# TensorE multiplies the identity by itself while it waits in three layer norms of a four-layer stack

## The chip, the cores and the metric

One NeuronCore of a Trainium2 chip runs the whole program in one launch. The metric is device time in microseconds (us), the median over runs.

## What is computed

Four layers act on x, 16 sequences of 256 tokens with 128 channels, in float32. Each layer normalises x, puts the result through a mixer s and a feed-forward part g, and adds the gated product:

```python
xn = _layernorm(x, axis=-1)
s = mixer(xn)          # delta rule, recurrence, local attention, causal attention
g = _silu(ffn(xn))     # layers 0 and 3: gated experts; 1 and 2: experts on chosen tokens
x = x + s * g
```

Layer 0's feed-forward part has an attention of its own, a norm (ln1), and eight experts of which the two best count. Layer 2 assigns tokens to eight experts by `norm @ centroids.T`. Layer 3 routes by `xt @ gate_w.T`. So three norms are followed at once by a product with a small routing matrix of 6 or 8 columns.

## The kernel before, in words

The program is a sequence of stages. `phase` opens a block in which each engine has its own list of instructions, and closes it with a barrier of all engines; engines wait for each other through semaphores (`wait_ge`, `then_inc`). 4096 tokens lie as 32 blocks of 128 (tokens on partitions); a norm takes them in 8 groups (GRP) of 4 blocks (GB).

`layer_norm` (L272) builds such a stage out of the class `Norm`. Per group: ACT opens the gate with silu (`open_gate`, L199) where the norm also adds the layer's product to x; DVE combines and takes statistics (`statistics`, L161 to L209); POOL takes the root (`root`, L215 and L216); DVE makes the bias (`centre`, L220); ACT normalises (`normalize`, L228, four instructions); TensorE transposes the four blocks into a PSUM bank, two banks in turn (`turn`, L243); ACT (`save_ch`, L248) or, with `columns`, DVE (`save_scaled`, L253) saves the bank to channel-major form; TensorE multiplies it with the routing matrix (`route`, L263); at the end DVE copies all logits (`save_logits`, L269). On TensorE the order is written out by hand: transposes of group g, then routing products of group g-1. On DVE it is statistics of g, bias of g-1, save of g-2.

Two of the three norms are calls of `layer_norm` with a router: **l0n1** (called at L1387, layer 0's ln1, on the attention's output, no gate, `columns` given, so DVE saves) and **norm3** (L2807, before layer 3, with gate; each group's input is waited for in `landed`). The third is **n2**, the function `norm_and_norm` (L339), before layer 2. It has the same structure with lines of its own: gates L463, statistics L379 and L382, POOL's first root L414 and L415 and second root L420 to L423 (two norms in a row are folded into one), bias L387, normalise L468, transposes L438, save L474, routing products L445, a small product for an offset (L450), and the first reader of the logits (L403).

A fourth routing norm, norm1, runs inside the last groups of layer 0's experts; it is built from `Norm` directly and isn't touched. Behind l0n1 come those experts (`experts`, up-products L555), behind n2 layer 2's mixer, behind norm3 layer 3's attention, which opens with projections (L2910, L2911, L2914). Ahead of l0n1 stands the output projection of layer 0's mixer (L1272). The scan of that mixer has transposes at L1028 and small products at L1039.

The PSUM banks of a norm are two for the transposes and one tile for the logits.

Of the kernel before, what the change touches and what calls it, by code (L numbers as in the profile page):

```python
# [13 lines left out]
P = 128  # L14
# [11 lines left out]
@contextmanager  # L26
def phase(nc, names, steps=1, spent=()):

    with ExitStack() as ctx:
        sems = [ctx.enter_context(nc.semaphore(n)) for n in names]
        step = ctx.enter_context(nc.Fori(0, steps)) if steps > 1 else 0
        with nc.Block() as block:
            yield block, step, sems
        numbers = sorted(s.num for s in sems + list(spent))
        while numbers:
            run = 1
            while run < len(numbers) and numbers[run] == numbers[0] + run:
                run += 1  # L40
            nc.sync.sem_clear(range(numbers[0], numbers[0] + run))
            numbers = numbers[run:]
        nc.all_engine_barrier()  # L43
# [118 lines left out]
    return dve.tensor_tensor(st.x[:, rows, :], st.x[:, rows, :], gate, ALU.add)  # L162


class Norm:


# [104 lines left out]
def layer_norm(nc, c, name, src, dst, dst_ch=None, gain=None, shift=None, combined=None, fetch=(), fetched=None, router=None,  # L272
# [2 lines left out]
    AHEAD = 2  # L275
    with ExitStack() as ctx:
        n = Norm(nc, ctx, c, name, src, dst, dst_ch, gain, shift, combined, router, ready, columns=columns)
        with phase(nc, [name + "_dve_step", name + "_pool_step"], spent=n.sems + list(spent)) as (block, _, (dve_step, pool_step)):
            if fetch:
                @block.sync  # L280
                def _(sp):
                    for to, what in fetch:
                        sp.dma_start(to, what).then_inc(fetched, 16)
# [27 lines left out]
            if dst_ch is not None:  # L311
                @block.tensor
                def _(pe):
                    for g in range(GRP + 1):
                        if g < GRP:
                            n.turn(pe, g)
                        if router is not None and g >= 1:
                            n.route(pe, g - 1)

            @block.scalar  # L320
            def _(act):
# [17 lines left out]
def norm_and_norm(nc, c, st, second, columns, cent, score, fetch, fetched, ready, ffn, ffn_fetched, landed):  # L339

    E = cent.shape[1]
    with ExitStack() as ctx:
# [7 lines left out]
        shifts = mem.sb("n2_shifts", [P, P])  # L350
        offset = mem.sb("n2_offset", [P, E])
        pt = [mem.psum(f"n2_pt{n}", [P, GB, P]) for n in range(2)]
        logits = mem.psum("n2_logits", [P, BLK, E])
        p_offset = mem.psum("n2_p_offset", [P, E])
        names = ["n2_" + n for n in ("gate_ready", "stats_ready", "first_ready", "second_ready", "bias_ready", "norm_ready", "turned",
                                     "ch_saved", "cent_ready", "offset_ready", "routed", "dve_step", "pool_step")]
        with phase(nc, names, spent=landed) as (block, _, sems):
# [73 lines left out]
            @block.tensor  # L431
            def _(pe):
                def turn(g):
                    pe.wait_ge(norm_ready, g + 1)
                    if g >= 2:
                        pe.wait_ge(ch_saved, g - 1)
                    for j in range(GB):
                        ins = pe.transpose(pt[g % 2][:, j, :], st.xn[:, g * GB + j, :], c.ident[:, :])  # L438
                    ins.then_inc(turned, 1)

                def route(g):
                    pe.wait_ge(ch_saved, g + 1)
                    for j in range(GB):
                        b = g * GB + j
                        ins = pe.matmul(logits[:, b, :], st.xnt[:, b * P:(b + 1) * P], scaled[:, :], start=True, stop=True)  # L445
                    ins.then_inc(routed, 1)

                pe.wait_ge(*ready)
                pe.wait_ge(cent_ready, 2)
                pe.matmul(p_offset[:, :], shifts[:, :], cent[:, :], start=True, stop=True).then_inc(offset_ready, 1)  # L450
                for m in range(GRP + 1):
                    if m < GRP:
                        turn(m)
                    if m >= 1:
                        route(m - 1)

            @block.scalar
            def _(act):
# [2884 lines left out]
```

## Time and profile before

| what | value |
|---|---|
| median of 3 runs | 2348.16 us (2347.99 to 2351.66) |
| the profiled execution's own time | 2353.4 us |
| its span, first to last instruction | 2351.7 us |
| mean granted TensorE clock | 0.901 |
| busy: PE, PEld, DVE, ACT, POOL | 2047.0, 1375.7, 1348.8, 1049.6, 625.4 us |

The profile is one execution. PE is TensorE's products and transposes, PEld its weight loads, DVE VectorE, ACT ScalarE, POOL GpSimd, SP the queue that issues DMAs. A timeline row gives start and length in us, engine, line of the kernel, operation, tile written and tiles read, shape, number of instructions merged, and in brackets the idle time of the engine before it with what ended it. A stretch row gives from and to in us, length, then busy time with the count of instructions for PE, PEld, DVE, ACT and POOL, the granted TensorE clock (1.00 is 2.4 GHz, 0.50 is 1.2 GHz), the DMA share and GB/s. The last matmul of a merged row is counted until its end, so that a row is somewhat longer than the engine's time for it.

### The profile page before, as it was taken

The numbers are of one execution on the slowest core, as the hardware profiler recorded it, in microseconds if no ns is written. First come the engines' busy times: TensorE is split into PE (matmuls) and PEld (weight loads), VectorE is DVE, ScalarE is ACT, GpSimd is POOL, SyncE is SP. The second block draws the span as 40 slices with busy tenths as digits, with TensorE's granted clock in tenths as the row PEclk, the third lists the DMA queues.
The fourth block names the chain that finished last, engine by engine and source line by source line (L and its number), as shares of the span: only waits on it lengthen the run. The fifth ranks groups of instructions, "written<-read, shape, count | busy, mean of one in ns | idle before, by whom it ended". The sixth has DMA issues, their size and how long they took to land. (4 is left out here: it accounts for less than half of the span.)

```text
span 2351.7 us, 46351 instructions
## 1 busy us (share of the span) xinstructions
PE 2047.0 (87%) x18079; PEld 1375.7 (59%) x18079; DVE 1348.8 (57%) x3508; ACT 1049.6 (45%) x2516; POOL 625.4 (27%) x720
## 2 busy tenths in 40 slices
PE   4989999977789999699847776858999999999898
PEld 2556666656666776454534443635666666666565
DVE  2027777734455555465348773124966767776677
ACT  3325655632244444212334334335666666666322
POOL 3016920011110000105650023362333333333100
PEclk9989999987869999799955566876999999999999
DMA  2034030021010000501240011340000000000000
GB/s 64 18 30 21 2 38 2 2 56 17 12 53 1 1 1 1 189 18 30 34 149 12 20 34 46 72 96 24 1 1 1 1 2 1 1 1 1 5 14 19
DMA packets 118327, 64.38 MB, mean 27 GB/s; under 512 B 65848, under 2 KB 113248, under 8 KB 116960
## 3 DMA queue, kind: packets, MB, share of 16 engines
q1 hardware_dynamic: 106128, 52.37, 9.6%
q0 software_dynamic: 11264, 8.66, 2.7%
q8 instruction: 146, 2.39, 0.4%
q14 instruction: 69, 0.57, 0.1%
q10 hardware_dynamic: 720, 0.40, 0.1%
HBM read 37.54 MB, written 23.86 MB: 26 GB/s over the span
## 5 line engine op out<-in xcount | busy, mean ns | idle before, releaser
L3000 ACT ACTIVATE l_prob<-l_ps,l_neg_max 128x128 f32<-128x128 f32 (+1 forms) x512 | 208.2, 419 | 50.0 <-DVE l_neg_max L3101 45.2
L1621 ACT ACTIVATE l0a_prob<-l0a_pst 128x1024 f32<-128x1024 f32 x128 | 131.0, 1023 | 119.9 <-PE l0a_pst L1539 119.9
L2885 POOL TENSOR_TENSOR l_prob<-l_prob,l_total 128x256 f32<-128x256 f32 x128 | 78.4, 612 | 371.8 <-DVE l_total L3109 371.8
L1672 DVE TENSOR_REDUCE l0a_peak<-l0a_ps 128x4 f32<-128x1024 f32 x128 | 156.2, 1221 | 15.5 <-PE l0a_ps L1534 13.4
L1534 PE MATMUL l0a_ps<-l0a_k,l0a_q 32*128 32x256 f32 x1024 | 146.0, 403 | 3.3 <-ACT l0a_prob L1621 2.5
L1539 PE MATMUL l0a_pst<-l0a_q,l0a_k 32*128 32x256 f32 x1024 | 145.8, 400 | 0.2 <-ACT l0a_prob L1621 0.2
L644 ACT ACTIVATE l0e_hidden<-l0e_ph,l0f_b 128x512 f32<-128x512 f32 x128 | 87.9, 687 | 129.1 <-PE l0e_ph L555 129.0
L3097 DVE TENSOR_TENSOR l_ps<-l_ps,future 128x512 f32<-128x512 f32 x128 | 89.4, 698 | 97.3 <-PE l_ps L2931 97.0
L565 PEld LDWEIGHTS l0e_py<-l0f_w,l0e_hidden 128*128 128x128 f32 x1024 | 119.7, 192 | 35.0 <-ACT l0e_hidden L644 32.8
L2886 POOL TENSOR_TENSOR l_prob<-l_prob,l_total 128x512 f32<-128x512 f32 x128 | 133.0, 1039 | 0.0
L565 PE MATMUL l0e_py<-l0f_w,l0e_hidden 128*128 128x128 f32 x1024 | 129.8, 280 | 0.3 <-ACT l0e_hidden L644 0.3
L555 PE MATMUL l0e_ph<-l0f_h_ch,l0f_w 128*128 128x512 f32 x256 | 125.1, 603 | 1.1 <-PEq L43 1.1
L2986 ACT ACTIVATE l_q<-l_px,l_bq 128x256 f32<-128x256 f32 x128 | 60.6, 473 | 144.1 <-PE l_px L2911 144.0
L3115 DVE COPY l_prob_t<-l_pt 128x768 f32<-128x768 f32 x128 | 119.3, 932 | 4.0 <-PE l_pt L2941 1.8
L1534 PEld LDWEIGHTS l0a_ps<-l0a_k,l0a_q 32*128 32x128 f32 x1024 | 91.3, 186 | 30.5 <-issue 22.7
L2941 PE MATMUL l_pt<-ident,l_prob 128*128 128x128 f32 x768 | 105.1, 273 | 3.4 <-POOL l_prob L2886 3.0
L3000 ACT ACTIVATION_READ_ACCUMULATOR l_prob<-l_ps,l_neg_max 128x1 f32 x512 | 104.1, 203 | 0.0
L2559 ACT ACTIVATE l_tanh<-l_tanh 128x1024 f32<-128x1024 f32 x64 | 66.8, 1057 | 81.1 <-DVE l_tanh L2614 81.1
L673 DVE SCALAR_TENSOR_TENSOR l0e_acc<-l0e_py,l0e_w,l0e_acc 128x128 f32<-128x128 f32 x192 | 54.1, 345 | 83.0 <-PE l0e_py L565 82.7
L2941 PEld LDWEIGHTS l_pt<-ident,l_prob 128*128 128x128 f32 x768 | 91.0, 141 | 16.3 <-POOL l_prob L2886 5.6
L2910 PE MATMUL l_px<-l_x,l_wq 128*128 128x256 f32 x256 | 90.5, 436 | 11.2 <-issue 5.6
L1539 PEld LDWEIGHTS l0a_pst<-l0a_q,l0a_k 32*128 32x128 f32 x1024 | 89.9, 184 | 1.5 <-issue 1.2
(518 smaller groups left out, 4833.6 us busy)
## 6 DMA issues: line engine op xcount, KB each, us to landing
l_band<-zero SPq DMA_DIRECT2D x16, 272.0 KB, 6.1
x_tok<-in_x_dram SPq DMA_DIRECT2D x2, 2048.0 KB, 7.9
l2f_w<-in_L_ffn_w_dram SPq DMA_DIRECT2D x2, 2048.0 KB, 9.8
l_rows<-l_band SPq DMA_DIRECT2D x16, 256.0 KB, 3.1
l1f_w<-in_L_ffn_W_dram SPq DMA_DIRECT2D x3, 1024.0 KB, 12.0
l2x_rows<-l2x_sent SPq DMA_DIRECT2D x8, 288.0 KB, 4.7
gd_tri<-gp_tri SPq DMA_DIRECT2D x8, 256.0 KB, 2.0
l0f_w<-gd_tri SPq DMA_DIRECT2D x8, 256.0 KB, 11.8
```

The costliest lines, as they stand in the source:

```text
L555: pe.matmul(ph1[u % 2][:, :], w1[:, unit, :], x, start=True, stop=True).then_inc(h1_ready, 1)
L565: ins = pe.matmul(py[x % 2][:, j, :], hidden[:, x % 2, f, j * P:(j + 1) * P], w2[:, (x % n_exp) * chunks + f, :], start=(f == 0), stop=(f ...
L1534: ins = pe.matmul(ps[m % 2][:, j, t, :], left, right, start=True, stop=True)
L1539: ins = pe.matmul(pst[:, j, t, :], left, right, start=True, stop=True)
L1621: act.activation(prob[:, (n // 2) % 2, pair, :, :].rearrange("p g t s -> p g (t s)"), pst[:, :, :, :].rearrange("p g t s -> p g (t s)"), A ...
L1672: dve.tensor_reduce(to, ps[m % 2][:, :, :, :], AX.X, ALU.max, negate=True).then_inc(max_ready, 1)
L2886: pool.tensor_tensor(far, far, total[:, m % 4, :, 1:2].to_broadcast([P, 2, 2 * P]), ALU.mult).then_inc(prob_ready, 1)
L2910: pe.matmul(px[:, 0:SEQ], wq[:, n, :], x, start=True, stop=True)
L2941: ins = pe.transpose(pt[:, h, j * P:(j + 1) * P], prob[:, m % 4, h, j * P:(j + 1) * P], c.ident[:, :])
L3000: act.activation(prob[:, m % 4, h, cols], ps[m % 2][:, h, cols], ACT.Exp, bias=neg_max[:, m % 4, h, t:t + 1], accum_out=total[:, m % 4, h, ...
L3097: dve.tensor_tensor(diag, diag, future, ALU.add).then_inc(masked, 1)
L3115: dve.tensor_copy(turned[:, n % 2, :, :], pt[:, :, 0:3 * P]).then_inc(turned_saved, 1)
```

## The change

A helper `keep_busy` issues a number of float32 products of the 128x128 identity with itself into a PSUM tile that nobody reads (`spare`, 128x128, new in each of the three stages). On TensorE's list of a routing `layer_norm` it stands 12 times at the start, then behind a wait for the first statistics 6 times, behind a wait for the first root 3 times, and behind each group's transposes and routing products 4 times (8 groups). In n2 it is 16 times at the start, 6 behind the first gate, 6 behind the first statistics, and 4 in each group. The added waits are for semaphores that are already counted up; nothing on the other engines changes.

```diff
--- before.py
+++ after.py
@@ -162,6 +162,11 @@
     return dve.tensor_tensor(st.x[:, rows, :], st.x[:, rows, :], gate, ALU.add)
 
 
+def keep_busy(pe, c, bank, count):
+    for _ in range(count):
+        pe.matmul(bank[:, :], c.ident[:, :], c.ident[:, :], start=True, stop=True)
+
+
 class Norm:
 
 
@@ -275,6 +280,7 @@
     AHEAD = 2
     with ExitStack() as ctx:
         n = Norm(nc, ctx, c, name, src, dst, dst_ch, gain, shift, combined, router, ready, columns=columns)
+        spare = Memory(nc, ctx).psum(name + "_spare", [P, P]) if router is not None else None
         with phase(nc, [name + "_dve_step", name + "_pool_step"], spent=n.sems + list(spent)) as (block, _, (dve_step, pool_step)):
             if fetch:
                 @block.sync
@@ -311,11 +317,19 @@
             if dst_ch is not None:
                 @block.tensor
                 def _(pe):
+                    if router is not None:
+                        keep_busy(pe, c, spare, 12)
+                        pe.wait_ge(n.stats_ready, 1)
+                        keep_busy(pe, c, spare, 6)
+                        pe.wait_ge(n.rstd_ready, 1)
+                        keep_busy(pe, c, spare, 3)
                     for g in range(GRP + 1):
                         if g < GRP:
                             n.turn(pe, g)
                         if router is not None and g >= 1:
                             n.route(pe, g - 1)
+                        if router is not None and g < GRP:
+                            keep_busy(pe, c, spare, 4)
 
             @block.scalar
             def _(act):
@@ -350,6 +364,7 @@
         shifts = mem.sb("n2_shifts", [P, P])
         offset = mem.sb("n2_offset", [P, E])
         pt = [mem.psum(f"n2_pt{n}", [P, GB, P]) for n in range(2)]
+        spare = mem.psum("n2_spare", [P, P])
         logits = mem.psum("n2_logits", [P, BLK, E])
         p_offset = mem.psum("n2_p_offset", [P, E])
         names = ["n2_" + n for n in ("gate_ready", "stats_ready", "first_ready", "second_ready", "bias_ready", "norm_ready", "turned",
@@ -445,6 +460,11 @@
                         ins = pe.matmul(logits[:, b, :], st.xnt[:, b * P:(b + 1) * P], scaled[:, :], start=True, stop=True)
                     ins.then_inc(routed, 1)
 
+                keep_busy(pe, c, spare, 16)
+                pe.wait_ge(gate_ready, 1)
+                keep_busy(pe, c, spare, 6)
+                pe.wait_ge(stats_ready, 1)
+                keep_busy(pe, c, spare, 6)
                 pe.wait_ge(*ready)
                 pe.wait_ge(cent_ready, 2)
                 pe.matmul(p_offset[:, :], shifts[:, :], cent[:, :], start=True, stop=True).then_inc(offset_ready, 1)
@@ -453,6 +473,8 @@
                         turn(m)
                     if m >= 1:
                         route(m - 1)
+                    if m < GRP:
+                        keep_busy(pe, c, spare, 4)
 
             @block.scalar
             def _(act):
```

## Rows read from the trace of the kernel before

**Rows 1.** Page, map of the span in 40 slices: TensorE's granted clock, tenths.
```profile
PEclk9989999987869999799955566876999999999999
```

**Rows 2.** Stretches of l0n1: length, busy us (instructions), clock, DMA share, GB/s.
```profile
661.30:665.40 4.10, 0.00 (x0) 0.00 (x0) 3.52 (x24) 0.97 (x3) 3.04 (x6) 1.00 0.72 224
...
666.10:687.80 21.70, 20.40 (x96) 19.82 (x96) 12.59 (x55) 11.34 (x28) 7.25 (x11) 0.50 0.10 41
688.80:692.70 3.90, 3.86 (x5) 1.28 (x5) 3.32 (x8) 2.35 (x4) 0.00 (x0) 0.50 0.57 200
692.70:696.10 3.40, 3.40 (x20) 2.58 (x21) 2.93 (x20) 1.29 (x2) 0.00 (x0) 1.00 0.30 64
```

**Rows 3.** Timeline, L1272 at half and full clock; then line L263's own answer.
```profile
652.18 1.91 PE L1272 MATMUL gr_py<-l_w_o,x_tok 128*128 128x128 f32 x8
...
656.29 3.74 PE L1272 MATMUL gr_ps<-l_w_o,x_tok 128*128 128x128 f32 x32
...
L263 PE MATMUL l0n_logits<-l0f_gw,l0f_h_ch x64: 221/361/362, 668.6 to 687.4; 128*128 128x8 f32 x64
```

**Rows 4.** Stretches of the scan around a rise of the clock (columns as in rows 2).
```profile
583.50:586.80 3.30, 2.91 (x84) 2.59 (x88) 1.18 (x3) 0.91 (x2) 0.00 (x0) 0.50 0.00 0
586.90:590.20 3.30, 3.02 (x121) 2.30 (x114) 0.00 (x0) 1.32 (x3) 3.09 (x3) 1.00 0.11 20
```

**Rows 5.** Timeline, TensorE before that rise.
```profile
583.89 1.12 PE L1028 MATMUL gr_px<-ident,gd_k_ch 128*128 128x128 f32 x4 [3.69 <-DVE gr_attn L1190]
...
585.79 1.70 PE L1039 MATMUL gr_pu<-gr_v_in,gr_inv 32*32 32x32 f32 x128
```

**Rows 6.** Timeline of l0n1: one steady group, and the stage's last copy.
```profile
676.01 1.12 PE L243 MATMUL l0n_pt<-ident,l0f_h_tok 128*128 128x128 f32 x4
...
677.17 0.81 DVE L253 TENSOR_SCALAR l0f_h_ch<-l0n_pt,l0f_columns 128x512 f32<-128x512 f32 x1 [0.44 <-PE l0n_pt L243]
...
678.49 1.09 PE L243 MATMUL l0n_pt<-ident,l0f_h_tok 128*128 128x128 f32 x4
...
687.77 0.42 DVE L269 COPY l0f_logits<-l0n_logits 128x256 f32<-128x256 f32 x1 [2.40 <-PE l0n_logits L263]
```

**Rows 7.** The groups of n2 as one stretch (columns as in rows 2).
```profile
1197.20:1217.30 20.10, 14.61 (x63) 12.80 (x63) 14.58 (x63) 13.21 (x30) 18.43 (x32) 0.50 0.41 170
```

**Rows 8.** Timeline of n2: first save, two steady groups, last transposes, first reader behind.
```profile
1200.62 0.57 ACT L474 ACTIVATE xn_ch<-n_pt 128x512 f32<-128x512 f32 x1
...
1211.10 1.11 PE L438 MATMUL n_pt<-ident,xn_tok 128*128 128x128 f32 x4 [1.19 <-ACT xn_tok L468]
...
1215.16 1.11 PE L438 MATMUL n_pt<-ident,xn_tok 128*128 128x128 f32 x4 [1.19 <-ACT xn_tok L468]
...
1222.44 1.12 PE L438 MATMUL n_pt<-ident,xn_tok 128*128 128x128 f32 x4 [0.59 <-ACT xn_tok L468]
...
1226.91 0.43 DVE L403 TENSOR_TENSOR l2f_score<-n_logits,l2f_second 128x256 f32<-128x256 f32 x1 [6.13 <-PE n_logits L445]
```

**Rows 9.** Stretches: norm3 before and in its groups; the opening of layer 3.
```profile
1571.90:1581.10 9.20, 0.00 (x0) 0.00 (x0) 6.84 (x25) 4.63 (x9) 3.61 (x4) 0.50 0.96 307
1581.10:1604.10 23.00, 21.32 (x96) 19.62 (x96) 14.07 (x64) 17.95 (x41) 12.26 (x13) 0.50 0.00 0
1605.70:1621.10 15.40, 10.32 (x17) 4.58 (x17) 1.45 (x3) 2.61 (x5) 0.21 (x1) 0.50 0.27 90
```

**Rows 10.** Timeline of norm3: the first root, the last normalise, the last copy.
```profile
1577.48 1.45 POOL L216 TENSOR_TENSOR norm_rstd<-norm_rstd,minus_half 128x4 f32<-128x4 f32 x1
...
1597.63 1.64 ACT L228 ACTIVATE norm_norm<-x_tok,norm_bias,norm_rstd 128x128 f32<-128x128 f32 x4
...
1604.12 0.36 DVE L269 COPY l3f_logits<-norm_logits 128x192 f32<-128x192 f32 x1 [6.97 <-PE norm_logits L263]
```

**Rows 11.** Timeline, layer 3's opening: the same projection early and later.
```profile
1605.72 1.19 PE L2910 MATMUL l_px<-l_x,l_wq 128*128 128x256 f32 x2 [1.64 <-POOL l_x L2878]
...
1625.27 0.70 PE L2910 MATMUL l_px<-l_x,l_wq 128*128 128x256 f32 x2
```

## The prediction

> **What bounds the kernel now.** I read the map of the span first. TensorE's granted clock is at nine tenths or more almost everywhere except in the scan, in the second layer (digits 5 to 8 of 10) and near the three norms of the change [rows 1]. Each of these norms is one short stage between two barriers, so its whole length lies on the path that sets the end, and a microsecond won or lost in it is won or lost in the kernel, unless the next stage takes it back.
>
> Then I read each norm by stretches. l0n1: TensorE is idle from 661.3 to 665.4 at full clock; it then has half clock from 666.1 to 687.8, where it is busy 20.4 of 21.7 us; it still has half clock for the first 3.9 us of the experts, and full clock only behind that [rows 2]. So here the slow TensorE is itself the bound. The price of its instructions comes from L1272, the same shape as the new product: eight instructions at half clock take 1.91 us from first start to last end, 32 at full clock 3.74 us. With one duration of 0.421 or 0.275 us taken off for the last, an instruction is (1.91 - 0.42)/7 = 0.213 us at half clock and (3.74 - 0.275)/31 = 0.112 us at full. A float32 product is two instructions: 32 routing products of l0n1 are 64 instructions [rows 3], while 32 transposes are 32. So a group of four blocks costs TensorE, at half and at full clock: transposes (4) 0.85 and 0.45 us; routing products (8, paced by their weight loads) 1.71 and 0.90 us; the four identity products of the change (8) 1.71 and 0.90 us.
>
> **Does the added work hold the clock?** It fell behind a stretch with no work, stayed down while TensorE was listed busy but mostly loading weights for eight columns, and rose behind back-to-back 512-column products [rows 2]. Identity products stream 128 columns per load and are dense like L1272, so I expect them to raise it. Do the transposes help to hold it? In the scan the clock rose from half to full at 586.9, and the stretch before it was eight transposes from 583.89 on and one microsecond of small products [rows 4, 5]. I take them as counting. The Trainium skill says otherwise (TensorE: Matmul & The Clock Gate, Part 4): full clock does not engage for transpose mode, which does not count as busy in the same way. By that rule the identity products would stand alone in each group and the norms would fall back to half clock; this trace speaks against it, through one rise only.
>
> **l0n1.** The stage is entered at full clock. Ahead of the first transposes stand 12 + 6 + 3 = 21 products, 42 x 0.112 = 4.7 us, from 661.4 to 666.1: the statistics and the root are ready long before their part of the list is over, so the list simply runs through and ends when the transposes were ready anyhow (666.1). Cost nothing, cover ends there to a tenth. In the groups TensorE paces the stage: transposes at 676.01 and 678.49 are 2.48 us apart, and DVE's save starts as they end [rows 6]. At full clock the group asks for 0.45 + 0.90 + 0.90 = 2.24 us. The other bound is the ring bias, ACT normalise, transposes, DVE save, statistics, bias, which now takes two groups (4.95 us) and loses 0.55 us: 2.2 us a group. Thus 2.24. The third group's transposes come 0.5 us earlier (670.6), five more groups at 2.24 give 681.8 for the eighth, and the tail is 0.45 + 0.90 + 0.90 + 0.90 + 0.2 = 3.35: 685.15 against the copy at 687.77 [rows 6]. **-2.6 us**. The first products of the experts may also be at full clock, but ACT's table load and softmax come between, so I count nothing.
>
> **n2.** The stage is at half clock, and POOL is the bound: 18.4 of 20.1 us [rows 7]. The list ahead is 28 products, 56 instructions: 12.0 us at half, 6.3 at full. Entered at 1189.4 and rising after the first few microseconds, it ends near 1198, against first transposes at 1197.2. That delay is hidden: ACT comes to the first save only at 1200.62 [rows 8]. In the steady groups, 4.06 us apart (1211.10 to 1215.16), TensorE at full clock would work 2.24 us and stand idle 1.8. I expect the clock to fall again within a few groups: idleness took it at 665.4 [rows 2], and here TensorE gets only short bursts. At half clock the group asks for 2.48 + 1.71 = 4.2 us, 0.1 more than POOL allows; over the groups after the fall the last transposes slip from 1222.44 to about 1224.0. Then the tail, which nothing hides: transposes 0.85, products 1.6, identity 1.71, products 1.6, end 0.2: 1229.9 against 1226.91 [rows 8]. **+3.0 us**. Had the clock held, the tail would be 0.45 + 0.90 x 3 + 0.2 from 1222.5, 1225.9: -1.0. These are the ends; I take the upper one, since the idle share is nearest to the stretches that lost the clock.
>
> **norm3.** Entered at half clock too. List: 12 + 6 = 18 products, at most 7.7 us from 1571.9, done by 1579.6 at worst; the three behind the root (1578.93) end at 1580.9 at worst, before the first transposes at 1581.1 [rows 9, 10]. Nothing is delayed. The groups are set by DVE and ACT, 2.69 us each; at full clock TensorE's 2.24 fits in with little idleness, so here I expect the clock to hold, about two to one. ACT's last normalise ends at 1599.27; transposes, products, identity, products at full clock are 0.45 + 0.90 x 3 + 0.2: 1602.65 against 1604.12 [rows 10]. **-1.4 us**. If the clock falls, each group takes 4.2 instead of 2.69, +1.5 us, until it rises.
>
> **Behind them.** Between a norm's end and the next products lie a copy and a barrier, over 1 us. The opening of layer 3 runs at half clock for 15.4 us and more with gaps [rows 9]; one projection is 1.19 us there and 0.70 later [rows 11]. I expect the clock to fall again soon, and count **-0.5 us**. No wait, semaphore or transfer is added; the spare bank is read by nobody; SP and POOL issue the same things, some of them earlier.
>
> Sum: -2.6 + 3.0 - 1.4 - 0.5 = **-1.5 us**. The profiled execution is 2353.4 us, its span 2351.7; the median of the runs shown is 5.2 us below it, at 2348.16. Applied to the median: **2346.7 us**, no change that can be told: 0.2%, 4.7 us, is about what a measurement of this kernel can tell from none.
>
> **Rivals.** (a) The clock holds in all three and into the stages behind. n2 then gives -1.0 instead of +3.0, layer 2's opening about -1, and layer 3's opening halves its chain of projections: six pairs at 0.49, three double-width ones at about 1.0, first scores 0.8, some -6.5 at the most. Together -2.6 - 1.0 - 1.4 - 1.0 - 6.5 = -12.5 us: 2335.7. With half of the openings it is 2340 or so. For: dense identity work. Against: the idle gaps. Chance 0.22.
>
> (b) Slower: the clock falls inside norm3 and n2 and the identity products themselves then make TensorE the bound. At 4.2 us a group instead of 2.69, seven groups of norm3 cost +10.4, the tail +1.7: +12.1; n2 +3.0; with l0n1 still won, +12.5 us: 2360.7. If only three groups of norm3 are run so: about +5. The point from which it decides: the clock falls at the first group of norm3, behind the gap between the list's end and the first transposes, and TensorE at half clock with a full queue does not get it back. The skill's rule on transposes would bring just this, and in l0n1 too (+13.7 there). Chance 0.15.
>
> (c) The change does not do what it says: multiplying a matrix of zeros and ones into a bank is not taken as work and the clock stays. Then l0n1 pays 8 x 1.71 = 13.7, n2's list lasts 12.0 us until 1201.4 and its seven groups 29 us, +10.5 in all with the tail, norm3 +12.1: +36 us, 2384. Nothing in the trace excludes it, as no instruction there has both operands the identity; the transposes, with one, speak against it. Chance 0.04.
>
> The forecast, with the mix varied (n2 kept or lost, norm3 kept or lost for a group or two), has 0.59.
>
> **Numbers.** Faster is (a) with a little of the forecast's edge: 0.24. Slower is (b), (c) and a little edge: 0.20. Same: 0.56. The range leaves out the deep end of (a) and the upper half of (b) with (c): 2340.0 to 2356.5. When the clock rises differs from execution to execution, and the runs of before already span 3.7 us, which the range must also hold.
>
> **What would show it.** Right: in l0n1 granted clock 1.00 from the list on, transposes 2.2 to 2.3 us apart, its copy 2.6 us earlier after its start; in n2 clock 1.00 from some microseconds after entry, then 0.50, L445 last ending 3 us later; in norm3 mostly 1.00, and the end 1.4 us earlier; half clock again in layer 3's opening. Wrong: spacing of 4.2 us in l0n1 or norm3 at 0.50 (b or c), identity instructions at 0.42 us each with no rise behind them (c), or projections of 0.70 us right at the start of layer 3 (a).

## The result, and the profile after

| | before | after |
|---|---|---|
| median of 20 runs each, one chip | 2348.95 us | 2344.43 us |
| lowest and highest | 2345.6 to 2353.5 | 2336.5 to 2354.1 |
| the profiled execution's own time | 2353.4 us | 2344.55 us |
| its span | 2351.7 us | 2342.8 us |
| mean granted clock | 0.901 | 0.915 |

The ratio is 0.9979 with an interval of 0.9969 to 0.9989. The kernel is faster, and by about as much (4.5 us between the medians, 0.2%) as I had called the least that can be told from nothing. The forecast was 2346.7 us, -1.5 us, within 2340.0 to 2356.5: right in sign, too small in size, and I had expected no change that can be told. One execution among those of the experiments below (experiment 3) took 9222.93 us and enters no mean and no interval. The changed kernel also spreads more: standard deviation 5.5 us against 2.4.

The page of the changed kernel first: busy time, and the map of the clock.

```profile
PE 2062.3 (88%) x18411; PEld 1397.5 (60%) x18411; DVE 1349.2 (58%) x3508; ACT 1049.6 (45%) x2516; POOL 625.6 (27%) x720
...
PEclk9989999987889999799975566988999999999999
```

TensorE has 332 instructions more than the 18079 of before. That is two for each identity product: 53 products in l0n1, 53 in norm3 and 60 in n2 are 166. The other engines have as many instructions as before. Against [rows 1] five digits of the map moved, by one or two. Two is the most: the 12th slice, with l0n1, the 21st, with n2, and the 28th, with the end of norm3 and layer 3's opening.

In the changed kernel the lines are shifted: the identity product is L167, the transposes of a `layer_norm` L248, its routing products L268, its last copy L274; in n2 the transposes are L453, the routing products L460, the first reader L418. The opening of layer 3 is L2932 and L2933.

**l0n1.** Timeline of TensorE after the change: the list, one steady group, the last routing products, the first product of the experts.

```profile
662.54 4.93 PE L167 MATMUL l0n_spare<-ident 128*128 128x128 f32 x42 [1.50 <-PEq L43]
...
676.23 0.64 PE L248 MATMUL l0n_pt<-ident,l0f_h_tok 128*128 128x128 f32 x4
676.71 0.96 PE L268 MATMUL l0n_logits<-l0f_gw,l0f_h_ch 128*128 128x8 f32 x8
677.52 1.14 PE L167 MATMUL l0n_spare<-ident 128*128 128x128 f32 x8
678.49 0.60 PE L248 MATMUL l0n_pt<-ident,l0f_h_tok 128*128 128x128 f32 x4
...
685.19 0.96 PE L268 MATMUL l0n_logits<-l0f_gw,l0f_h_ch 128*128 128x8 f32 x8
687.25 1.19 PE L577 MATMUL l0e_ph<-l0f_h_ch,l0f_w 128*128 128x512 f32 x1 [1.10 <-PEq L43]
```

And the stretches of the same stage: list, groups, first products of the experts.

```profile
662.40:667.30 4.90, 4.76 (x42) 4.79 (x43) 3.85 (x26) 1.84 (x5) 3.67 (x8) 1.00 0.84 298
667.30:686.20 18.90, 18.26 (x162) 17.88 (x160) 12.59 (x55) 11.17 (x28) 7.07 (x11) 1.00 0.09 36
687.25:690.50 3.25, 3.25 (x4) 1.15 (x4) 2.73 (x7) 1.82 (x3) 0.00 (x0) 0.50 0.57 179
```

The clock is 1.00 from the list to the copy, where [rows 2] showed 0.50. Groups are 2.26 us apart here (678.49 less 676.23), where [rows 6] showed 2.48. TensorE has two thirds more instructions per group (20 instead of 12) and is still through earlier. The experts start at 0.50 as before: here nothing is carried over the barrier.

**n2.** The stretches of the changed kernel: before the rise, from the rise to the fall, at half clock again, and after a second rise.

```profile
1184.90:1188.90 4.00, 3.97 (x19) 4.00 (x20) 3.21 (x11) 1.67 (x3) 0.50 (x1) 0.51 0.93 217
1188.90:1202.50 13.60, 11.10 (x93) 10.24 (x92) 11.89 (x49) 9.13 (x22) 12.01 (x20) 1.00 0.90 349
1202.50:1212.80 10.30, 10.27 (x48) 9.98 (x48) 6.33 (x29) 5.76 (x13) 9.55 (x16) 0.50 0.01 2
1212.80:1221.40 8.60, 7.49 (x62) 6.89 (x61) 0.41 (x4) 4.85 (x11) 6.13 (x14) 1.00 0.00 0
```

The timeline shows the groups in the middle stretch 4.58 and 4.26 us apart, the second and third with no idle time before their transposes, and a later one at full clock with idle time again:

```profile
1202.53 1.12 PE L453 MATMUL n_pt<-ident,xn_tok 128*128 128x128 f32 x4 [1.01 <-ACT xn_tok L490]
...
1207.11 1.06 PE L453 MATMUL n_pt<-ident,xn_tok 128*128 128x128 f32 x4
...
1211.37 1.06 PE L453 MATMUL n_pt<-ident,xn_tok 128*128 128x128 f32 x4
...
1217.93 0.66 PE L453 MATMUL n_pt<-ident,xn_tok 128*128 128x128 f32 x4 [0.68 <-ACT xn_tok L490]
...
1221.40 0.42 DVE L418 TENSOR_TENSOR l2f_score<-n_logits,l2f_second 128x256 f32<-128x256 f32 x1 [5.13 <-PE n_logits L460]
```

The last row answers to the last of [rows 8]: VectorE now waits 5.13 us for the logits where it waited 6.13. That microsecond is the stage's gain.

**norm3.** Stretches of the changed kernel: full clock, half clock, full clock again, and the opening of layer 3.

```profile
1567.70:1578.00 10.30, 6.91 (x54) 6.02 (x53) 9.89 (x42) 6.25 (x15) 7.57 (x8) 1.00 0.46 171
1578.00:1584.80 6.80, 6.80 (x35) 6.80 (x34) 6.56 (x32) 6.47 (x15) 5.09 (x6) 0.50 0.00 0
1584.80:1596.10 11.30, 11.29 (x101) 11.20 (x101) 2.57 (x12) 7.14 (x17) 3.22 (x4) 1.00 0.01 1
1597.70:1612.10 14.40, 9.54 (x16) 4.02 (x16) 1.45 (x3) 2.45 (x5) 0.22 (x1) 0.53 0.28 96
```

Timeline, transposes on both sides of the fall and the rise, then the first two projections of layer 3:

```profile
1578.99 1.06 PE L248 MATMUL norm_pt<-ident,norm_norm 128*128 128x128 f32 x4
...
1583.26 1.06 PE L248 MATMUL norm_pt<-ident,norm_norm 128*128 128x128 f32 x4
...
1586.24 0.60 PE L248 MATMUL norm_pt<-ident,norm_norm 128*128 128x128 f32 x4
...
1588.46 0.60 PE L248 MATMUL norm_pt<-ident,norm_norm 128*128 128x128 f32 x4
...
1597.72 0.67 PE L2932 MATMUL l_px<-l_x,l_wq 128*128 128x256 f32 x2 [1.64 <-POOL l_x L2900]
...
1600.33 1.19 PE L2932 MATMUL l_px<-l_x,l_wq 128*128 128x256 f32 x2 [1.27 <-ACT l_q L3008]
```

One group cost 4.27 us (1578.99 to 1583.26) where the engines ahead need 2.69; with the clock back, the next ones run 2.2 us apart and win back a part of it. One projection of layer 3 still gets full clock (0.67 us, the later one 1.19 as in [rows 11]).

**Where the time went.** I cut both executions at the same events: first statistics and last copy of l0n1; first down-product of the experts; first gate and first reader (L403 before, L418 after) of n2; first gate and last copy of norm3; first mask of layer 3's attention.

| stretch, us | before | after | difference |
|---|---|---|---|
| start to l0n1 | 661.41 | 662.42 | +1.01 |
| l0n1 | 26.37 | 23.76 | -2.61 |
| opening of the experts | 5.82 | 5.78 | -0.04 |
| experts, norm1 and layer 1, to n2 | 495.83 | 492.94 | -2.89 |
| n2 | 37.49 | 36.49 | -1.00 |
| behind n2 to norm3 (layer 2) | 346.41 | 343.67 | -2.74 |
| norm3 | 30.80 | 31.06 | +0.26 |
| opening of layer 3 | 20.62 | 19.74 | -0.88 |
| the rest | 726.9 | 726.9 | 0.0 |

The stages that the change touches, with the opening of layer 3, give -4.2 us; the two stretches of nearly 500 and 340 us between them, in which nothing was changed, give -5.6. The spans of the profiled executions are 8.85 us apart and the medians 4.5, since the profiled execution of before was 4.4 us slower than its own median. So one pair of traces can't say whether -2.89 and -2.74 belong to the change.

### The profile page after: what moved, and what is told of

The parts are those of the page before. It is cut to its first block and busy times, and to the rows that moved or that the text cites. A ratio compares the mean times of both kernels' runs of the same rounds, so it can differ in the third digit from the quotient of the medians.

```text
span 2342.8 us, 47015 instructions
## 1 busy us (share of the span) xinstructions
PE 2062.3 (88%) x18411; PEld 1397.5 (60%) x18411; DVE 1349.2 (58%) x3508; ACT 1049.6 (45%) x2516; POOL 625.6 (27%) x720
## 5 line engine op out<-in xcount | busy, mean ns | idle before, releaser
L2932 PE MATMUL l_px<-l_x,l_wq 128*128 128x256 f32 x256 | 90.0, 433 | 11.2 <-issue 5.6
```

What stands on the lines that cost most here:

```text
L2932: pe.matmul(px[:, 0:SEQ], wq[:, n, :], x, start=True, stop=True)
```

## The experiments

Two theories went into them. The first: a norm is worth what its own stage shows, l0n1 -2.6, n2 -1 or +3, norm3 between +0.3 and -1.4, and what lies between them is chance. The rival (B): by ending a norm earlier the change shifts all that follows against the moments at which the clock changes, and that brings a gain of its own. The twelve kernels ran in three groups (1 to 4, 5 to 8, 9 to 12), each group on another chip and beside runs of the kernel before on the same chip (medians 2349.65, 2318.54 and 2317.14 us). The table behind experiment 12 has all of them. The interval belongs to the ratio; the difference of the plain means, given beside it, doesn't always agree with the ratio to the last digit.

**1. The products in l0n1 alone.**

```diff
-                    if router is not None:
+                    if router is not None and name in ['l0n1']:
                         keep_busy(pe, c, spare, 12)
...
-                            keep_busy(pe, c, spare, 4)
+                            keep_busy(pe, c, spare, {'l0n1': 4, 'norm3': 0}[name])
...
-                keep_busy(pe, c, spare, 16)
...
-                    if m < GRP:
-                        keep_busy(pe, c, spare, 4)
```

> The identity products in l0n1 alone. Theory A (the won time is TensorE's full clock in l0n1, where half clock was the bound): from the first statistics to the copy of the logits 23.8 us instead of 26.4, granted clock 1.00 between, n2 and norm3 as before at 0.50; time 2.6 us lower (ratio 0.9989). Rival B (the three norms only shift the later stages against the clock's own rhythm, and the gain comes from there): the l0n1 stage is 2.6 us shorter, but the median moves by the whole 4 to 5 us, or not at all.

Measured: 2344.22 us against 2349.65, ratio 0.997 (0.996 to 0.998), -5.4 us. The stage took 23.77 us, -2.60, as in the whole change. n2 and norm3 are back at 37.49 and 30.80. So this norm alone brought as much as all three, and twice what its stage shows.

**2. The products in n2 alone** (no list and no group products in l0n1 and norm3).

```diff
-                    if router is not None:
+                    if router is not None and name in []:
                         keep_busy(pe, c, spare, 12)
...
-                            keep_busy(pe, c, spare, 4)
+                            keep_busy(pe, c, spare, {'l0n1': 0, 'norm3': 0}[name])
```

> The identity products in n2 alone. Theory A: the stage, 37.5 us from first gate to first reader of the logits, becomes 36.5 if the clock is at 1.00 as the last transposes run, and about 40.5 if it is at 0.50; over runs a mean near 0 to +1.5 us, ratio 1.000 to 1.0006. Rival B: it is always 1 us or more shorter, since full clock is regained in time in every execution (ratio 0.9995).

Measured: ratio 1.0004 (0.9992 to 1.0017), mean difference -0.1 us. In its profiled execution the stage took 36.51 us, the -1.0 of the whole change again; the clock rose at 1191.7, fell at 1205.4, rose at 1215.6. If every run had had that, the mean would be -1.0; the interval holds it, and zero.

**3. The products in norm3 alone** (`name in ['norm3']`, counts 0 and 4, none in n2).

> The identity products in norm3 alone. Theory A: the stage, 30.8 us from first gate to copy, is 29.4 if the clock holds and 31 or more if it falls between the list and the first groups; layer 3's opening 0.5 to 1 us shorter; ratio 0.9995 to 1.000. Rival B: the clock at the end of norm3 carries into layer 3's opening and takes 3 us or more from its 20.6 us: ratio 0.9985.

Measured: ratio 1.0011 (0.9999 to 1.0023). But in the profiled execution the clock held from the list to the end of the stage. Its stretch, and VectorE's last copy:

```profile
1567.40:1594.70 27.30, 22.05 (x180) 20.24 (x180) 18.41 (x79) 19.63 (x45) 16.04 (x18) 1.00 0.13 47
```
```profile
1592.90 0.36 DVE L274 COPY l3f_logits<-norm_logits 128x192 f32<-128x192 f32 x1 [5.73 <-PE norm_logits L268]
```

The stage took 29.56 us, -1.24, near the -1.4 of the prediction. VectorE waited 5.73 us, against 6.97 in [rows 10]. The runs as a whole show no gain (+1.3 us in the mean). That this norm has at least two outcomes is shown by this trace beside that of the whole change (31.06); how often each comes, no run here tells.

**4. The lists ahead of the groups, without the group products**, in all three norms.

```diff
-                            keep_busy(pe, c, spare, 4)
+                            keep_busy(pe, c, spare, {'l0n1': 0, 'norm3': 0}[name])
...
-                    if m < GRP:
-                        keep_busy(pe, c, spare, 4)
```

> The lists at the start of the three norms stay, the four products in each group are left out. Theory A (transposes and routing products alone don't hold the clock, the products in the groups do): l0n1 falls back to 0.50 within its first groups and is 25 to 26 us long instead of 23.8; n2 and norm3 fall back too but cost nothing: 37 and 30 us. Ratio 0.9995 to 0.9998. Rival B (the transposes and routing products are enough once the clock is up): l0n1 at 1.00 to its end, about 22.5 to 23 us, norm3 28.5 us; ratio 0.998 or lower, better than the whole change.

Measured: ratio 1.0003 (0.9994 to 1.0013). Stretches of l0n1 in this kernel:

```profile
662.00:674.90 12.90, 8.87 (x76) 8.29 (x74) 9.38 (x49) 6.53 (x17) 6.96 (x12) 1.00 0.44 164
675.00:686.00 11.00, 10.74 (x52) 10.74 (x53) 6.82 (x32) 6.73 (x17) 3.80 (x6) 0.50 0.01 1
```

and its transposes behind the fall:

```profile
677.78 1.12 PE L248 MATMUL l0n_pt<-ident,l0f_h_tok 128*128 128x128 f32 x4
...
680.25 1.09 PE L248 MATMUL l0n_pt<-ident,l0f_h_tok 128*128 128x128 f32 x4
```

The list holds the clock for the first three groups; then it falls and the spacing is 2.47 us, that of [rows 6]. The stage took 25.55 us, -0.8 only. In n2 the clock rose at 1197.2 and fell at 1204.1, in norm3 it rose at 1579.5 and fell at 1586.4, and both stages had their old lengths (37.49, 30.81). The group products are needed.

**5. l0n1's groups without the list** (on the second chip, as experiments 6 to 8; n2 and norm3 without products in all four).

```diff
-                    if router is not None:
+                    if router is not None and name in []:
                         keep_busy(pe, c, spare, 12)
...
-                            keep_busy(pe, c, spare, 4)
+                            keep_busy(pe, c, spare, {'l0n1': 4, 'norm3': 0}[name])
```

> l0n1 with the four products in each group but without the list at its start, n2 and norm3 untouched. Theory A (TensorE idle ahead of the first transposes loses the clock, and at half clock the identity products are one more load on the engine that bounds the stage): clock 0.50 from about 3 to 5 us after the stage's start, groups 4.2 us apart until the clock rises again, the stage 30 to 40 us instead of 26.4, time 3 to 13 us higher. Rival B (a saturated TensorE gets the clock back at once): stage 26 to 27 us, time as before.

Measured: ratio 0.9995 (0.9984 to 1.0007), stage 28.82 us, +2.45. Timeline of its transposes:

```profile
669.48 1.06 PE L248 MATMUL l0n_pt<-ident,l0f_h_tok 128*128 128x128 f32 x4
...
673.74 1.06 PE L248 MATMUL l0n_pt<-ident,l0f_h_tok 128*128 128x128 f32 x4
...
678.01 1.06 PE L248 MATMUL l0n_pt<-ident,l0f_h_tok 128*128 128x128 f32 x4
...
681.03 0.60 PE L248 MATMUL l0n_pt<-ident,l0f_h_tok 128*128 128x128 f32 x4
...
683.25 0.60 PE L248 MATMUL l0n_pt<-ident,l0f_h_tok 128*128 128x128 f32 x4
```

The clock fell at 666.0, before the first transposes (666.86). Then two groups cost 4.26 us each, the price of rival (b), and a third 3.02; at 679.7, in that one, the clock came back, and the groups ran 2.22 us apart. The stage lies between both expectations (30 to 40, or 26 to 27 us). Rival (b)'s price is right. Its last clause, that TensorE at half clock with a full queue does not get the clock back, is not borne out here; experiment 11 has a case for it.

**6. l0n1 without the products of its last group.** TensorE's last identity products stand ahead of the last routing products, on the path.

```diff
-                        if router is not None and g < GRP:
-                            keep_busy(pe, c, spare, 4)
+                        if router is not None and g < GRP - 1:
+                            keep_busy(pe, c, spare, {'l0n1': 4, 'norm3': 0}[name])
```

> The identity products in l0n1 alone, but none in the last group, where they stand ahead of the last routing products. Theory A: the tail is 0.9 us shorter, the stage 22.9 us instead of 23.8, the clock at 1.00 to its end; time 0.5 to 1 us below the l0n1-only kernel. Rival B (the clock falls before the experts start and their opening loses it again, or the shift brings the fall of the clock in layer 1 back): stage 22.9, but time the same or higher.

Measured: 2315.33 against 2318.54, ratio 0.999 (0.998 to 1.0001), mean difference -3.6 us. Stage 23.06 us: -3.3, that is 0.7 more than with them. VectorE's copy waits 1.15 us instead of 1.77:

```profile
685.16 0.42 DVE L274 COPY l0f_logits<-l0n_logits 128x256 f32<-128x256 f32 x1 [1.15 <-PE l0n_logits L268]
```

**7. A pause behind l0n1 in the kernel before.** Experiment 1 had brought 2.8 us more than its stage. For the rival this is the shift. So four fillings (memsets) of a spent tile on VectorE, which compute nothing, put the experts later without touching the norm.

```diff
                 if router is not None:
                     n.save_logits(dve)
+                if name == "l0n1":
+                    for _ in range(4):
+                        link(dve.memset(n.stats[:, :, :, :], 0.0))
```

> The kernel before with four idle memsets of 192 columns on DVE behind l0n1's last copy, which lengthen that stage by an estimated 0.8 to 1.0 us and compute nothing. Theory A (a shortened stage is worth its own length and no more): time 0.8 to 1.0 us higher. Rival B (it also matters when the program reaches layer 1, for in the kernel before the clock falls there at 1054.5 for 6.8 us and costs 3.4 us, and in the profiled executions of the l0n1-only kernel and of the whole change it doesn't): with the program 0.9 us later against the clock's changes the fall in layer 1 goes away, the stretch from the experts' first down-product to n2's first gate is 493 instead of 496 us, and the time is 1 to 2.5 us lower although only waiting was added.

Measured: ratio 1.0004 (0.9995 to 1.0013), mean difference +0.9 us. The timeline of VectorE shows the pause:

```profile
688.55 0.42 DVE L269 COPY l0f_logits<-l0n_logits 128x256 f32<-128x256 f32 x1 [2.40 <-PE l0n_logits L263]
688.97 1.19 DVE L304 MEMSET l0n_stats<- 128x192 f32 x4
691.02 0.43 DVE L703 TENSOR_TENSOR l0e_prob<-l0f_logits,l0f_gb 128x256 f32<-128x256 f32 x1 [0.87 <-PEq L43]
```

From the copy to the experts' first work it is 2.47 us instead of 1.06, but the opening as a whole (copy to first down-product) took 8.10 instead of 5.82: the clock rose at 697.1 only, behind all six up-products ahead of the first down-product, and by the rows these take the missing 0.9 us (5.84 us for the six instead of 4.93). I had sized this pause by its fillings alone. By stages the kernel should be 2.3 us slower, which the interval (-1 to +3 us) also holds. So the runs show no gain from the shift, but they don't exclude one of a microsecond or two.

**8. The products in l0n1, and a pause of twelve fillings** (experiment 1's kernel with the loop of experiment 7, `range(12)`). If the surplus came from the shift, undoing the shift should take it away, and more.

> The identity products in l0n1 alone, and twelve such memsets behind the stage's last copy, estimated 2.4 to 3.0 us, so that the experts start when they did in the kernel before. Theory A: 2.4 to 3.0 us above the l0n1-only kernel, about 2347, and layer 1 as there, 493 us. Rival B: the fall of the clock in layer 1 is back, 496 us, and the time is that of the kernel before, 2348 to 2350, with its wider spread.

Measured: 2322.83 against 2318.54, ratio 1.0014 (1.0004 to 1.0025), mean difference +3.2 us. The stage took 23.68 us, the opening 10.70. By stages that is -2.69 + 4.88 = +2.2 us. The rest, 1 us, is within the interval.

**9. The short pause** (two fillings; on the third chip, as experiments 10 to 12).

> The kernel before with two memsets behind l0n1's last copy, 0.7 us by the 0.35 us that each of the four took in the pause of 1.4 us. Theory A: 0.7 us above the kernel before. Rival B (place against the clock's changes decides): the rise of the clock in the experts' opening is 1.3 to 2.4 us ahead of the first down-product instead of 0.6 to 1.8, where the profiled executions had no fall in layer 1 near 1054, so that stretch is 493 us and the median 0.5 to 2.5 us below the kernel before.

Measured: ratio 1.0005 (0.9995 to 1.0016), mean difference +0.2 us; opening 7.40 us, +1.6, of which 0.8 is the pause. No shift that I tried made the kernel faster.

**10. Experiment 1 again, on the third chip.**

> The identity products in l0n1 alone, a second time, beside the whole change on the same chip. Theory A: 2.6 us below the kernel before (ratio 0.9989). Rival B: 4 to 6 us below again (0.9975 to 0.9982), the surplus from layer 1, and as low as the whole change or lower.

Measured: 2316.63 against 2317.14, ratio 0.9994 (0.9984 to 1.0004), mean difference -1.3 us. The stage took 23.77 us once more. So the stage is the same to a hundredth, while the gain of the whole kernel was -5.9 us (mean) there and -1.3 here, with intervals that don't meet.

This trace also answers a question of the prediction. Its clock did not fall behind l0n1: it stayed at 1.00 through the experts' opening, and the opening took the same 5.78 us. TensorE ran its first four up-products in 1.96 us (3.58 at half clock in the changed kernel), and then waited for ScalarE:

```profile
691.08 1.13 PE L570 MATMUL l0e_ph<-l0f_h_ch,l0f_w 128*128 128x512 f32 x2 [1.81 <-ACT l0e_hidden L659]
```

**11. The whole change again.**

> The whole change, a second time. Theory: 3 to 5 us below the kernel before (ratio 0.998), its spread over the executions wider than that of the l0n1-only kernel, since in n2 and norm3 the clock is held in some executions and falls in others; 0 to 2 us above the l0n1-only kernel. Rival: it is below the l0n1-only kernel by the 1.0 us that n2 won in its profile.

Measured: 2316.05 (2303.5 to 2321.7), ratio 0.999 (0.9976 to 1.0004), mean difference -2.3 us, a little less than the 3 to 5 expected; it isn't told apart from experiment 10. Its profiled execution shows the other outcome of n2. Stretches first, then the timeline of the last groups and the first reader:

```profile
1189.70:1210.20 20.50, 16.08 (x132) 14.56 (x131) 16.13 (x69) 12.77 (x29) 18.45 (x29) 1.00 0.60 233
1210.20:1226.60 16.40, 15.81 (x75) 15.41 (x73) 2.93 (x13) 6.98 (x16) 9.71 (x19) 0.50 0.00 0
```
```profile
1216.25 1.06 PE L453 MATMUL n_pt<-ident,xn_tok 128*128 128x128 f32 x4
...
1220.51 1.06 PE L453 MATMUL n_pt<-ident,xn_tok 128*128 128x128 f32 x4
...
1222.93 2.05 PE L167 MATMUL n_spare<-ident 128*128 128x128 f32 x8
1224.78 1.72 PE L460 MATMUL n_logits<-n_scaled,xn_ch 128*128 128x8 f32 x8
```
```profile
1226.64 0.42 DVE L418 TENSOR_TENSOR l2f_score<-n_logits,l2f_second 128x256 f32<-128x256 f32 x1 [9.10 <-PE n_logits L460]
```

Here the clock held until 1210.2 and then stayed down to the end: groups 4.26 us apart, identity products between the last two routing steps at 0.50, and VectorE waits 9.10 us. TensorE had no idle time from 1211.92 to 1226.50, and the clock did not come back in these 14.6 us. The stage took 40.46 us, +3.0 against 37.49. norm3 held its clock this time (29.57).

**12. Experiment 6 again.**

> The products in l0n1 alone, none in its last group, a second time, now on the same chip as the other two. Theory A: 0.7 to 0.9 us below the l0n1-only kernel, the lowest of the four. Rival B: no difference that can be told from it, or above it.

Measured: 2314.51 against 2317.14, ratio 0.9991 (0.9981 to 1.0001), mean difference -2.6 us, stage 23.05. It lies 1.2 us below experiment 10 in the mean, as theory A has it (0.7 to 0.9), but within the noise.

All of them. n2 without products is 37.5 in all but two traces (experiments 6 and 10: 38.5, where some of POOL's first instructions took longer), norm3 without products is 30.8 in all:

| kernel | ratio (interval) | mean, us | l0n1 | experts' opening | to n2 | n2 | norm3 |
|---|---|---|---|---|---|---|---|
| before, trace | | | 26.37 | 5.82 | 495.83 | 37.49 | 30.80 |
| after | 0.9979 (0.9969 to 0.9989) | -5.0 | 23.76 | 5.78 | 492.94 | 36.49 | 31.06 |
| 1 l0n1 | 0.997 (0.996 to 0.998) | -5.9 | 23.77 | 5.78 | 492.89 | 37.49 | 30.80 |
| 2 n2 | 1.0004 (0.9992 to 1.0017) | -0.1 | 26.37 | 5.78 | 493.09 | 36.51 | 30.79 |
| 3 norm3 | 1.0011 (0.9999 to 1.0023) | +1.3 | 26.38 | 5.78 | 492.89 | 37.52 | 29.56 |
| 4 lists | 1.0003 (0.9994 to 1.0013) | +1.7 | 25.55 | 6.32 | 496.05 | 37.49 | 30.81 |
| 5 groups | 0.9995 (0.9984 to 1.0007) | -0.1 | 28.82 | 6.78 | 494.23 | 37.47 | 30.78 |
| 6 no last | 0.999 (0.998 to 1.0001) | -3.6 | 23.06 | 5.78 | 493.36 | 38.53 | 30.78 |
| 7 pause | 1.0004 (0.9995 to 1.0013) | +0.9 | 26.37 | 8.10 | 495.21 | 37.48 | 30.78 |
| 8 l0n1, pause | 1.0014 (1.0004 to 1.0025) | +3.2 | 23.68 | 10.70 | 495.36 | 37.49 | 30.78 |
| 9 short pause | 1.0005 (0.9995 to 1.0016) | +0.2 | 26.35 | 7.40 | 494.82 | 37.49 | 30.79 |
| 10 as 1 | 0.9994 (0.9984 to 1.0004) | -1.3 | 23.77 | 5.78 | 495.54 | 38.50 | 30.78 |
| 11 whole | 0.999 (0.9976 to 1.0004) | -2.3 | 23.67 | 5.78 | 493.33 | 40.46 | 29.57 |
| 12 as 6 | 0.9991 (0.9981 to 1.0001) | -2.6 | 23.05 | 5.86 | 495.86 | 37.49 | 30.80 |

**Chance between the norms.** The column "to n2" has values from 492.9 to 493.4 and from 494.2 to 496.1, with no order in the kernels: experiment 1 has the first, its repetition the second. The stretch that makes the difference is in layer 1. The same window of the kernel before and of experiment 3, neither of which changes anything there, first by stretch:

```profile
1054.50:1061.40 6.90, 6.90 (x10) 3.09 (x11) 3.00 (x16) 0.00 (x0) 1.51 (x2) 0.51 0.09 22
```
```profile
1054.50:1061.40 6.90, 6.16 (x48) 3.11 (x46) 4.40 (x22) 2.15 (x4) 2.30 (x3) 1.00 0.08 20
```

then one group of products in each timeline:

```profile
1056.24 6.20 PE L1882 MATMUL l_p_x<-xn_ch,l_w_x 128*128 128x512 f32 x8
```
```profile
1053.79 3.15 PE L1897 MATMUL l_p_x<-xn_ch,l_w_x 128*128 128x512 f32 x7
```

In the first the clock fell for 6.9 us and eight products took 6.20 us; in the second seven took 3.15. Such a fall is in the traces of before and of experiments 4, 7, 8, 6's repetition (12), 9 and 10, and not in those of after and of 1, 2, 3, 5, 6 and 11; in 7 to 10 it lasted 3.4 us. It is worth 1.5 to 3 us, as much as the whole forecast was about. Experiments 7 and 8 have it, as the rival wanted, but experiment 10 has it too, with l0n1 shortened and no pause. Layer 3 has a similar place (0 or 1.4 to 2.8 us, experiments 3 and 4 among others).

Layer 2 is less steady still. From n2 to norm3 it took 336 to 346 us in the traces of the first chip (experiments 1 to 4), and 307 to 311 on the other two chips. The waits of TensorE between 1398 and 1440 us show where, first in experiment 1, then in experiment 10, which is the same kernel:

```profile
PE l_ps L2450 <- issue: 14.5, 9, 3.5
```
```profile
PE l_ps L2450 <- ACT l_tanh L2574: 3.5, 11, 0.8
```

On the first chip TensorE stood idle there although it waited for nothing that the profile shows. Such gaps of over 0.7 us add up to 13 to 22 us between about 1403 and 1443 in each trace of experiments 1 to 4, and to 21 and 22 us in the traces of before and after; in the eight traces of the other chips there is none. What causes them isn't shown. They are a large part of the 30 us between the chips, and differ by 8 us from trace to trace on one of them.

## Why the prediction was right or wrong, point by point

**l0n1: right.** -2.6 predicted, -2.61 measured, and -2.60 in both runs of this part alone (experiments 1 and 10). Each term held: the list is 4.93 us for 42 instructions (4.7 predicted, with 0.28 for the last one's duration), the products took 1.14 us with the last one's duration (0.90 without, as predicted), the groups 2.2 to 2.3 us. The list costs next to nothing: the first transposes come 4.89 us behind the first statistics instead of 4.72. Experiments 4 and 5 show that both parts are needed, since the list keeps the clock over the entry and the group products keep it afterwards. The last group's identity products stood in my tail with 0.90 us, and I didn't ask whether they were worth it: 0.7 us on the path, which experiments 6 and 12 give back. That I counted nothing for the experts' opening was right too: in experiment 10 it had full clock and took no less time.

**The identity is taken as work: right.** Rival (c) fell in all traces that have a list; in n2 the clock rose 4.0 us after the list began (1184.9 to 1188.9), where TensorE had stood idle at 0.50 before the change.

**Do transposes hold the clock?** I took them as counting. In norm3 of experiments 3 and 11 the clock held with four transposes, eight routing and eight identity instructions in each 2.69 us; in experiment 4, with the identity instructions left out, it fell. The Trainium skill (TensorE: Matmul & The Clock Gate, Part 4) says that full clock does not engage for transpose mode, which does not count as busy in the same way. The falls of experiment 4 fit that rule. By my reading of it l0n1 should have fallen to half clock with 13.7 us to pay even with the identity products, and it didn't; but since these are in all the runs that held, no run here separates transposes from the rest.

**n2: the mechanism right, the value taken open.** I gave two ends, -1.0 and +3.0, and took the upper one, as the clock would fall in the groups. It does fall in the groups in each trace that has the products. The failed step is that I let it stay down "over the groups after the fall", into the tail. After a fall at 1202.5 it was back at 1212.8, in time for the tail, and the stage came to -1.0; after a fall at 1210.2 it was still down when the stage ended 16.4 us later, and the stage came to +3.0. So what the clock is in the tail decides which end is taken, and three traces gave -1.0, -1.0 and +3.0. Why it stayed down there is open: TensorE worked for 14.6 us without a gap, longer than the 10.3 us that it took to come back in the other case. A term between the ends would have been the better one. Experiment 2's runs (1.0004, with both -1.0 and zero in the interval) agree.

**norm3: the same.** If it held, I said -1.4, and it gave -1.2 twice. In the execution of the changed kernel it fell for 6.8 us, and I had said +1.5 us per group until it rises. Three spacings grew (3.42, 4.27 and 2.98 us from 1575.57 to 1586.24), which lost 2.6 us against 2.69 each; the three behind them were 2.22 us and won 1.4 back. The stage came to +0.26, 1.5 us above the held one. That catching up was missing from my price.

**Behind them: right in kind.** In the changed kernel the clock fell 0.9 to 2.4 us after each stage's end (687.1 for a copy at 686.19, 1223.0 for 1221.40, 1598.5 for a copy near 1596.1); experiment 10 is the exception, behind l0n1. The opening of layer 3 gave -0.9 where the clock fell 2.4 us after norm3's copy, and -0.15 and 0.0 in experiments 3 and 11, where it fell 1.8 and 1.5 us after it. -0.5 was a fair value. That also refutes rival (a): no trace shows the projections at 0.50 a pair throughout.

**The sum.** With the values of this trace it is -2.6 - 1.0 + 0.3 - 0.9 = -4.2, which is the measured 4.5 to 5.0 within its interval (2.6 to 7.3 us); with those of experiment 11 it is -2.7 + 3.0 - 1.2 + 0.0 = -0.9, against a mean of -2.3 on that chip, again within the interval. My -1.5 lies between. (Two sums of mine are off by a tenth or two: norm3's tail gives -1.5 by its terms, and rival (b)'s seven groups +10.6.) The mis-sized terms are n2 (by 4 us in the profiled execution) and norm3 (by 1.7 the other way). That the total still came out within 3 us is in part luck: the two errors have opposite signs, and the unchanged layers move by more than the whole sum. Of the signs that I named, those for l0n1 came; in this trace n2 ended 1.0 us earlier instead of 3 later, and norm3 took 0.3 us more instead of 1.4 less.

**What stays open.** l0n1 alone gave -5.9 on one chip and -1.3 on another with the same stage. Its variant without the last group gave -3.6 and -2.6 on two chips. The mean of the four is -3.4, and by their stages it would be -3.0; so on the whole the theory of stages fits. But in experiment 1 the stage's -2.6 lies outside the interval (-9.4 to -4.7 us), and the shift that the rival wanted brought no gain that shows in the three forms tried (experiments 7, 8, 9). That chip is the one with TensorE's gaps in layer 2. Whether these react to the earlier end of l0n1 or it was chance isn't settled, and since the traces of before and after have the same gaps, that holds for a part of the 4.5 us too. Nor is the whole change told apart from its l0n1 part: neither n2 nor norm3 alone shows a gain, each tried on one chip only. The version of experiments 6 and 12 has the best stage for l0n1, -3.3 us, and a ratio at or below 0.9991 twice, with half the spread of the whole change (standard deviation 2 to 3 us against 5). It is the one I would keep, though its lead over the whole change isn't shown: they differ by less than their intervals.

## What to carry to other kernels

In this kernel filling TensorE's waits paid where TensorE at half clock was itself the bound of a short stage that is entered at full clock; there both the entry and each gap needed filling, and nothing should be filled ahead of the last result. Where another engine was the bound, the filler brought 1.2 us at best and cost 3 us where the clock was down in the tail, because at half clock it made TensorE the bound. Gains of 2 or 3 us are to be read from the stage, in several executions, since the unchanged parts of the same program vary by as much.

## What the runs showed of the hardware that I had not expected

The clock came back in the middle of a stage, under a mix of transposes, routing and identity products that kept TensorE busy nearly all the time at 0.50: 10.3 us after the fall in n2 (1202.5 to 1212.8), 6.8 us in norm3 (1578.0 to 1584.8), 13.7 us in experiment 5 (666.0 to 679.7). In n2 of experiment 11 the same mix did not bring it back in the 16.4 us to the stage's end. Why isn't known. A late entry into work can prolong half clock: with the experts 1.4 us later the clock rose at 697.1, and their opening took 2.3 us longer.

Whole stretches that no change touches move by 2 to 3 us from execution to execution through one short fall of the clock (0.51 for 6.9 us in layer 1), and the chips themselves differ: the kernel before has medians of 2349.65, 2318.54 and 2317.14 us on three of them, with layer 2 at 336 to 346 us in traces of the first, where TensorE stands idle without a wait that the profile shows, and 307 to 311 us in those of the other two.
